# The last attention of a four-layer network: two passes made one slotted loop, with sums on TensorE and rounding on GpSimd

## The reference, cut to what matters

```python
q = (x @ Wq + bq).reshape(1, B * N, H, hd)
kv = (cond @ Wkv + bkv).reshape(1, -1, 2, H, hd)
q = _fq_sym(q * scale, axis=-1); k = _fq_sym(k, axis=-1); v = _fq_sym(v, axis=2)
attn = softmax(einsum('bhqd,bhkd->bhqk', q, k))
attn = _fq_unsigned(attn, axis=-1)      # s = max / 255, round(attn / s) * s
out = einsum('bhqk,bhkd->bhqd', attn, v)
return out.reshape(B, N, C) @ Wp + bp
```

## Time and profile before

| what | value |
|---|---|
| runs | 3636.0, 3638.04, 3641.99 us; median 3638.04 |
| the profiled execution's own time | 3633.23 us |
| its span, first to last instruction | 3631.5 us |
| first pass (from the first maximum) | 2589 to 2880 us |
| between the passes | 2880 to 2897 us |
| second pass | 2897 to 3197 us |
| end of the stage | 3220 us |

### The profile page before, as it was taken

The page is one execution under the profiler, slowest core; times in us unless marked ns, Lnnn a source line. Parts: engine busy times, 40 slices in busy tenths (PEclk is TensorE's granted clock), DMA queues, the critical chain, the costliest instruction groups (busy, mean ns, idle before and its releaser), DMA issues. The chain is left out here.

```text
span 3631.5 us, 49639 instructions
## 1 busy us (share of the span) xinstructions
PE 2993.6 (82%) x15375; PEld 1889.5 (52%) x15378; DVE 2276.1 (63%) x5414; ACT 1692.8 (47%) x3312; POOL 263.4 (7%) x323
## 2 busy tenths in 40 slices
PE   7887977787789999824999999726799899957899
PEld 4334645565567777612777777514211244434576
DVE  5664346767777777674444444477999866657532
ACT  4451224565655555411222222203699999934322
POOL 0010002111121111000000000040000000001200
PEclk9898987999999999956999999867655555567899
DMA  1002030000000000003000000001000000020000
GB/s 53 1 2 79 0 127 1 24 1 1 1 1 7 7 1 1 1 31 116 1 1 1 0 0 0 18 0 41 1 0 0 0 1 0 0 88 2 2 1 12
DMA packets 32878, 56.37 MB, mean 16 GB/s; under 512 B 5248, under 2 KB 24640, under 8 KB 30144
## 3 DMA queue, kind: packets, MB, share of 16 engines
q1 hardware_dynamic: 32704, 54.24, 4.3%
HBM read 52.99 MB, written 1.05 MB: 15 GB/s over the span
## 5 line engine op out<-in xcount | busy, mean ns | idle before, releaser
L2482 ACT ACTIVATE a_v_all<-psum,a_ln 128x1024 f32<-128x1024 f32 x256 | 283.9, 1114 | 14.7 <-PE psum L2421 9.3
L2536 DVE TENSOR_REDUCE a_half_max<-psum 128x1024 f32 x256 | 289.7, 1242 | 0.0
L2399 PE MATMUL psum<-a_ks,a_qs 96*128 (+1 forms) x512 | 263.6, 620 | 27.2 <-ACT psum L2468 16.8
L2468 ACT ACTIVATE psum<-psum,a_half_max 128x1024 f32<-128x1024 f32 x256 | 278.4, 1088 | 3.7 <-DVE a_half_max L2536 3.3
L2421 PE MATMUL psum<-a_qs,a_ks 99*128 (+1 forms) x512 | 263.6, 618 | 5.0 <-ACT a_qs L2474 1.2
L2559 DVE TENSOR_SCALAR a_probs<-a_v_all 128x1024 bf16<-128x1024 f32 x256 | 177.6, 694 | 122.6 <-ACT a_v_all L2482 110.2
L1581 ACT ACTIVATE a_normed<-psum,a_head_bias,a_head_scale 128x128 f32<-128x128 f32 x448 | 168.2, 457 | 160.5 <-DVE a_head_bias L1724 160.4
L1473 PE MATMUL psum<-a_probs_t,a_vals 128*128 128x256 f32 x768 | 202.5, 402 | 19.5 <-ACT a_probs_t L1599 19.5
L843 DVE SCALAR_TENSOR_TENSOR f_silu<-f_silu,psum 128x352 f32<-128x352 f32 (+2 forms) x88 | 50.4, 573 | 244.6 <-ACT f_silu L818 244.5
L1744 DVE TENSOR_REDUCE a_neg_max<-psum 128x2 f32<-128x512 f32 (+1 forms) x128 | 122.2, 955 | 124.4 <-PE psum L1453 123.9
L1453 PE MATMUL psum<-a_k_t,a_q_t 128*128 128x256 f32 (+1 forms) x512 | 194.1, 503 | 0.0
(11 more groups left out here) (465 smaller groups left out, 6407.1 us busy)
## 6 DMA issues: line engine op xcount, KB each, us to landing
a_w_raw<-in_L_xattn_wproj_dram SPq DMA_DIRECT2D x2, 2048.0 KB, 14.1
a_ctx_t<-in_ctx_t_dram SPq DMA_DIRECT2D x8, 512.0 KB, 5.4
f_w_silu<-in_L_ffn_gate_dram SPq DMA_DIRECT2D x1, 2112.0 KB, 9.6
f_w_mul<-in_L_ffn_up_dram SPq DMA_DIRECT2D x1, 2112.0 KB, 14.2
a_probs<-in_ctx_t_dram SPq DMA_DIRECT2D x4, 512.0 KB, 5.3
f_w_silu<-in_L_ffn_Wu_dram SPq DMA_DIRECT2D x1, 2048.0 KB, 8.0
f_w_mul<-in_L_ffn_Wg_dram SPq DMA_DIRECT2D x1, 2048.0 KB, 12.6
f_w_down<-in_L_ffn_Wd_dram SPq DMA_DIRECT2D x1, 2048.0 KB, 17.6
```

What stands on the lines that cost most here:

```text
L2399: mm = pe.matmul(core.bank(4 * (t % 2) + 2 * half + c), qs[0:KS, bass.ds(h * TOK + t * P, P)], ks[0:KS, bass.ds(h * CTX + (2 * half + c) * ...
L2468: act.activation(banks, banks, ACT.Exp, bias=half_max[:, half, at], accum_out=half_sums[:, half, at]).then_inc(summed, 1)
L2482: act.activation(exps[:, k % 4, :], core.bank(2 * (k % 2), 2), ACT.Exp, bias=ln255[:, :]).then_inc(exp_ready, 1)
L2536: v.tensor_reduce(half_max[:, half, bass.ds(h * NT + t, 1)], core.bank(4 * (t % 2) + 2 * half, 2), AX.X, ALU.max, negate=True).then_inc(ma ...
```

## The change

The two passes become one loop of 285 slots, written out in full. In slot s:

- TensorE makes the scores of pair s (128 queries by 1024 keys) into a ring of two double banks (banks 0 to 3). VectorE takes their negated maximum. ScalarE does not touch them.
- After a head's 16 pairs VectorE splits its 128 x 8 maxima into three parts. Two slots later TensorE transposes them at once (one transpose, through the same ring), VectorE copies the row block to `max_rows`, and SP writes it with three DMAs into `qs`.
- TensorE makes the logits of pair s - 21 (two key tiles by 512 queries) into two single banks (4 and 5), each as soon as the exponential before last has left it. ScalarE takes two exponentials of 128 x 512 in place of one of 128 x 1024, into a ring of 12 buffers.
- GpSimd rounds both to bf16 (128 x 1024 in one instruction), into a ring of 4.
- Every second slot TensorE takes a group of four key tiles. Four f32 matmuls with `one_row` (17 columns, a one in the last) add the exponentials' sums, and four bf16 matmuls with the values add the weighted values, all into bank 6, key tile u at the column tile 32u.
- After four groups (a chunk of 512 queries) ScalarE copies bank 6 to `out_t`; TensorE turns it with four f32 matmuls against `select` (which also adds the four column tiles); VectorE takes the reciprocal of the sum and multiplies twice.

GpSimd now also scales, rounds and clamps the values. ScalarE waits for that before its first exponential, since `v_all` and the exponentials share their space. Before the loop VectorE builds `select` and zeroes bank 6, and TensorE waits for that.

```diff
+        UNITS, PAIRS, TILES_PER = 12, 4, 4
+        PER = 2 * NT
+        LAG = PER + 5
+        SLOT_COUNT = LAG + H * PER + 8
+        RING, LOGITS, OUT, TURNED = 0, 4, 6, 7
...
 @block.sync
+                for h in range(H):
+                    sp.wait_ge(rows_kept, h + 1)
+                    if h >= 2:
+                        sp.wait_ge(ROWS_IN[h % 2], 48 * (h // 2))
+                    for part in range(3):
+                        sp.dma_start(qs[KS + part:KS + part + 1, h * TOK:(h + 1) * TOK].rearrange("a (t n) -> a t n", t=NT),
+                                     max_rows[part * NT:(part + 1) * NT, h % 2, :]).then_inc(ROWS_IN[h % 2], 16)
...
 @block.gpsimd
+                g.wait_ge(v_inv_ready, 1)
+                g.tensor_tensor(v_all[:, :, :], v_all[:, :, :], v_inv[:, :].unsqueeze(1).broadcast_to([P, KT, D]), ALU.mult).then_inc(v_step, 1)
+                g.wait_ge(v_step, 1)
+                g.tensor_scalar(v_all[:, :, :], v_all[:, :, :], ROUND, ROUND, ALU.add, ALU.subtract).then_inc(v_step, 1)
+                g.wait_ge(v_step, 2)
+                g.tensor_scalar(v_int[:, :, :, 0:DH], v_all[:, :, :].rearrange("p k (h d) -> p k h d", h=H), 127.0, -127.0,
+                                ALU.min, ALU.max).then_inc(v_ready, 1)
+                for m in range(H * PER):
+                    g.wait_ge(exp_ready, 2 * m + 2)
+                    at_least(g, weighted_done, (m - PAIRS) // 2 + 1)
+                    first = 2 * m % UNITS
+                    g.tensor_scalar(probs[:, m % PAIRS, :], exps[:, first:first + 2, :].rearrange("p u n -> p (u n)"),
+                                    ROUND, ROUND, ALU.add, ALU.subtract).then_inc(probs_ready, 1)
...
 @block.tensor
+                def rows(h):
+                    pe.wait_ge(ring_free, ring_use["rows", h] - 1)
+                    pe.wait_ge(parts_ready, h + 1)
+                    pe.transpose(ring(("rows", h)).bitcast(BF16)[0:3 * NT, 0:P], max_parts[:, h, :, :].rearrange("p s t -> p (s t)"),
+                                 core.ident_bf[:, :]).then_inc(ring_full, 1)
+
+                def logits(m):
+                    h, (c, j) = m // PER, divmod(m % PER, KT // 2)
+                    if m % PER == 0:
+                        pe.wait_ge(ROWS_IN[h % 2], 48 * (h // 2 + 1))
+                    for u in range(2):
+                        key = 2 * j + u
+                        at_least(pe, exp_ready, 2 * m + u - 1)
+                        pe.matmul(core.bank(LOGITS + u), ks[0:KM, h * CTX + key * P:h * CTX + (key + 1) * P],
+                                  qs[0:KM, h * TOK + c * QC:h * TOK + (c + 1) * QC], start=True, stop=True).then_inc(logits_full, 1)
+
+                def group(g):
+                    n, i = divmod(g, GROUPS)
+                    h, c = divmod(n, CH)
+                    if g == 0:
+                        pe.wait_ge(v_ready, 1)
+                    if i == 0:
+                        at_least(pe, out_kept, n)
+                    pe.wait_ge(exp_ready, TILES_PER * (g + 1))
+                    for u in range(TILES_PER):
+                        pe.matmul(core.bank(OUT)[32 * u:32 * u + W, :], one_row[:, :], exps[:, (TILES_PER * g + u) % UNITS, :],
+                                  start=(i == 0), stop=False, skip_group_check=True)
+                    pe.wait_ge(probs_ready, 2 * (g + 1))
+                    for u in range(TILES_PER):
+                        mm = pe.matmul(core.bank(OUT)[32 * u:32 * u + W, :], v_int[:, TILES_PER * i + u, h, :],
+                                       probs[:, (2 * g + u // 2) % PAIRS, u % 2 * QC:(u % 2 + 1) * QC],
+                                       start=False, stop=(i == GROUPS - 1), skip_group_check=True)
+                    mm.then_inc(weighted_done, 1)
+
+                for s in range(SLOT_COUNT):
+                    if s < H * PER:
+                        scores(s)
+                    if rows_slot(s) is not None:
+                        rows(rows_slot(s))
+                    if pair_at(s) is not None:
+                        logits(pair_at(s))
+                    if group_at(s) is not None:
+                        group(group_at(s))
+                    if chunk_at(s, 4) is not None:
+                        turn_heads(chunk_at(s, 4))
...
 @block.scalar
-                            act.activation(banks, banks, ACT.Exp, bias=half_max[:, half, at], accum_out=half_sums[:, half, at]).then_inc(summed, 1)
+                def exponential(m):
+                    for u in range(2):
+                        n = 2 * m + u
+                        act.wait_ge(logits_full, n + 1)
+                        at_least(act, weighted_done, (n - UNITS) // TILES_PER + 1)
+                        act.activation(exps[:, n % UNITS, :], core.bank(LOGITS + u), ACT.Exp, bias=ln255[:, :]).then_inc(exp_ready, 1)
...
 @block.vector
+                for s in range(SLOT_COUNT):
+                    if s < H * PER:
+                        maxima(s)
+                        if s == 2:
+                            scale_values()
+                        if s % PER == PER - 1:
+                            split(s // PER)
+                    if rows_slot(s) is not None:
+                        keep_rows(rows_slot(s))
+                    if chunk_at(s, 4) is not None:
+                        keep_heads(chunk_at(s, 4))
```

More of the change, by code:

```diff
@@ L2269, in layer3_attention @@
     CH = TOK // QC
-    GROUP = 2
-    GROUPS = KT // GROUP
+    W = DH + 1
     LEAST = 1e-8
@@ L2309, in layer3_attention @@
[L2309 to L2324, removed]
@@ L2392, in _ @@
                 pe.wait_ge(proj_free, TILES)
-                def scores(h, t):
-                    for half in range(2):
-                        at_least(pe, summed, 2 * (h * NT + t) + half - 3)
-                        for c in range(2):
-                            mm = pe.matmul(core.bank(4 * (t % 2) + 2 * half + c), qs[0:KS, bass.ds(h * TOK + t * P, P)],
-                                           ks[0:KS, bass.ds(h * CTX + (2 * half + c) * BANK, BANK)], start=True, stop=True)
-                        mm.then_inc(scores_ready, 1)
@@ L2438, in _, with scores @@
-                v_int_flat = v_int[:, :, :].rearrange("p k d -> p (k d)")
-                steps(pe, step)
+                pe.wait_ge(loop_ready, 1)
+                def scores(s):
+                    h, (t, half) = s // PER, divmod(s % PER, 2)
+                    n = ring_use["scores", s]
+                    if n >= 2:
+                        pe.wait_ge(ring_free, n - 1)
+                    for c in range(2):
+                        mm = pe.matmul(ring(("scores", s))[:, c * BANK:(c + 1) * BANK], qs[0:KS, h * TOK + t * P:h * TOK + (t + 1) * P],
+                                       ks[0:KS, h * CTX + (2 * half + c) * BANK:h * CTX + (2 * half + c + 1) * BANK], start=True, stop=True)
+                    mm.then_inc(ring_full, 1)
@@ L2577, in _ @@
-                v.drain()
-                for t in range(NT):
-                    one = heads[:, t, :].rearrange("p (h d) -> p h d", h=H)
-                    v.tensor_tensor(one, one, sums[:, :, t].unsqueeze(2).broadcast_to([P, H, DH]), ALU.mult).then_inc(out_ready, 1)
+                v.tensor_tensor(select[:, :], core.ident[:, 0:W], core.ident[:, 32:32 + W], ALU.add)
+                v.wait_ge(stack_free, 2 * TILES)
+                v.memset(core.bank(OUT), 0.0)
+                for u in range(2, TILES_PER):
+                    v.drain()
+                    last = v.tensor_tensor(select[:, :], select[:, :], core.ident[:, 32 * u:32 * u + W], ALU.add)
@@ new lines, in _ @@
+                for s in range(SLOT_COUNT):
+                    if s < H * PER:
+                        maxima(s)
[7 more added lines that the diff above has]
+                        keep_heads(chunk_at(s, 4))
+                v.drain().then_inc(out_ready, NT)
```

205 lines of the change are left out of this document (95 added, 110 removed).

## The result

The changed kernel takes 3989.7 us (median of 4 runs, 3988.4 to 3991.9) against 3638.0 before: 1.0966 times as long, 95% interval 1.0947 to 1.0985. The forecast was 3533, range 3455 to 3600, faster with 0.89: wrong in sign and outside its range. The profiled execution has a span of 3986.7 us.

The account below looks back on a forecast made before the run. VectorE filled the first pass, ScalarE most of the second. New stage: 2.7 + 27.7 + 416 + 32.6 + 19 + 3 + 3 + 4.2 = 508.2 against 612.8 us, 104.6 less; median 3533, range 3455 to 3600.

Parts of the forecast that it names:

- GpSimd's term: New loop, per slot: one GpSimd rounding of 128x1024 taken at 1.04 us plus 0.07 hand-over, bounds 1.04 and 2.34.
- rival 3: Loop: GpSimd's rounding costs like its two-input operation, 2.34 + 0.07, so every slot is 2.41; 3679 us, chance 0.07.
- The prediction's sentence on the Trainium skill: GpSimd rounding: some 2.6 cycles per element, estimated 2.2 us for 1024, against the move; one-or-two-operation bodies about one cycle.
- the stage: Last attention, first maximum to first transpose of the finished heads: 612.8 us before, forecast 508.2, so 104.6 less.
- Lead: Loop's start: 21 slots with maxima alone before the first logits, 27.7 us; GpSimd's value scaling, 17.7, covered.
- Chain of two slots: Loop: in-order queues from one odd exponential's end through TensorE to the next take 3.54 us, 1.77 a slot.
- Heads: Starts of 16 heads: split 1.15, waits for the row bank, and VectorE-GpSimd hindrance 0.6 each; 16 x 1.2 = 19 us.
- Turning a chunk: Finished chunks, 32 times: f32 transposes hold TensorE's queue some 0.5 us, costing 0.1 a chunk, 3 in all.
- rival 2: Values' sums: bf16 column tiles go one after the other, +0.66 every two slots, +84; 3617 us, chance 0.06.
- rival 4: TensorE through the loop: clock stays at 1.2 GHz, 195 us more; median 3728, chance 0.04.
- Rival 1: Loop: ScalarE is the bound at 1.54 us a slot, 181 less; median 3457, chance 0.13.
- the break-even: GpSimd's rounding in the loop: the change turns slower from 2.25 us a slot, an instruction of 2.18.

Follow-up runs that it names:

- experiment 1: Kernel before the change, with 26 GpSimd instructions of 128x1024 in various forms added beside the first pass to price each; 3632.7 us in its one run.
- experiment 2: Changed kernel with GpSimd copying the exponentials to bf16 in place of rounding them to whole numbers; 3577.4 us, ratio 0.9838.
- Experiment 9: Kernel with VectorE's rounding and scores between a pair's logits, with the values' add and subtract also moved from GpSimd to VectorE; 3543.7 us, ratio 0.9748.
- experiment 7: Changed kernel with the rounding on VectorE one slot later, and additionally the scores moved between the two logits of a pair; 3552.2 us, ratio 0.9770.
- experiments 6: Kernel with GpSimd copying instead of rounding, with the next scores moved between the two logits of a pair; 3569.8 us, ratio 0.9821.
- 8: Kernel with GpSimd copying instead of rounding, without TensorE's f32 set of sums (denominators from converted values); 3546.0 us, ratio 0.9743.
- experiment 5: Kernel with GpSimd copying instead of rounding, copying only 8 columns of each pair; 3545.7 us, ratio 0.9752.
- 3: Changed kernel with the rounding moved from GpSimd to VectorE, one slot later; 3563.9 us, ratio 0.9789.
- experiment 12: Copying kernel without sums, splits and heads' last product on GpSimd, values rounded on VectorE; then rows one slot, logits two slots later; 3442.7 us, ratio 0.9467.

## Why the prediction was wrong

**The step that failed is GpSimd's term**, "one input and constants resembles the cast: I take 1.04". It measured 3.63 alone (experiment 1), and one every 3.60 in the loop, outside bounds of 1.04 and 2.34 that both came from rows of other operations. Putting 3.60 in rival 3, whose mechanism is what happened, gives 3679 + 256 x (3.60 - 2.41) + 13 for the longer lead = 3997, against 3989.7. Its chance of 0.07 rested on those bounds, and its own price, 2.34 + 0.07, was too low as well.

The prediction's sentence on the Trainium skill, "GPSIMD Engine Reference", section 3.1, leaned the right way by luck. The section gives its 2.6 cycles for two inputs, and about one cycle per element for bodies of up to two operations, an estimate of 0.9 us for 1024 elements. The limits, multiply-and-add and the copies, at 1.04 to 1.05, lie near that; add-and-subtract at 3.63 and the single operations at 2.77 do not, and there the trace decides.

**The rest, judged by experiment 2, where GpSimd costs the 1.04 assumed:** the stage measures 556.6 us against 508.2.
- Lead: 40.3 against 27.7, +12.6. GpSimd's scaling was taken at 17.7 and "covered", to show from 4 us more. It took 26.45, mis-sized by the same operation (14.04). Its end, at 2629.2 in the changed kernel, was still 7.9 us before the first exponential; what it delayed was the first split in VectorE, whose steps waited beside it, and with that the turned row. Experiment 9 takes 6.4 off experiment 7's lead. (The lead's terms, as listed, add to 27.5, not 27.7.)
- Chain of two slots: 3.54 against 3.70. The mechanism holds: experiments 6 and 8 shorten it by 0.36 and by 0.87. Two sizes were off. The f32 set is 0.87, not 0.44: the earlier trace rows was read as eight sets of four, but an f32 matmul leaves two records, so 32 records are four sets. Exponentials back to back start 0.58 to 0.59 apart (the row of three in experiment 2), not 0.73. Together +0.43 and -0.29 make +0.14 of the 0.16 measured: one error hid two thirds of the other.
- Heads: hindrance was taken at 0.6 a head within bounds of 0 and 3.1; experiment 5 makes it 35.5 / 16 = 2.2. The nearest row had been one subtraction beside one select. Beside full copies the two conversions of a split take 1.05 and 0.86 instead of 0.17, and the chunks' product, not among the steps counted, 1.01 instead of 0.23, 32 times.
- Turning a chunk holds TensorE 0.8 to 0.96 us (eight records again), not 0.5.
- Right: the bf16 tiles lie side by side (four in 0.40), against rival 2; the clock is 0.95 to 1.00 in experiments 2, 3 and 5, against rival 4; the first maximum starts 2.4 us behind the reduction's end (2594.1), against 2.6; the end is 4.8 behind the last exponential's start.
- Rival 1, ScalarE as the bound: experiment 12 comes near it, with 1.47 us a pair and ScalarE busy for 88%.

What "would show it" named GpSimd over 90% busy, TensorE waiting before the bf16 set and small steps of over 1 us; all three came.

Open: why GpSimd's price depends so on the operations named. The runs give the prices and no reason for them.

## What to carry to other kernels

Before a step is moved to another engine, price that very operation there: rows of a cast and of a two-input operation, 1.04 and 2.34, lay on either side of the break-even and yet both below the 3.63 that it costs, 3.5 times the value taken. Small VectorE steps of 0.17 us beside GpSimd's instructions can each come to about 1 us, beside 1.04 and beside 3.63 alike (1.64 at most), and to 5.53 beside the long ones at the start, so count every one of them, and move them too. And when work is taken from TensorE, look at its waits again: with less to do, its clock fell behind them, and two slots of slack gave back what the removal had promised.

## What the runs showed that I had not expected

- On GpSimd, for 128x1024 f32: copy 1.04 us, both limits 1.04, multiply-and-add 1.05, add, subtract or multiply alone 2.77, add-and-max and add-and-subtract 3.63. VectorE does the last in 0.68.
- Steps of 8 columns on VectorE, two-input or conversions alike, lasted 2.52, 3.60 and 5.53 us beside GpSimd's long instructions at the start and 0.86 to 1.05 beside copies of 1.04. Beside the loop's roundings of 3.63 none lasted longer than 1.64: some of the casts ended 0.03 us behind a rounding's end, most of the other steps that were held about 1.05 us into a rounding, and the step of 5.53 ended 11.47 us into an instruction of 14.04. The maxima out of PSUM keep their 1.22.
- TensorE's granted clock fell from 1.00 to 0.50 behind its waits of 1.29 and 2.43 us, though it was busy again at once, and was back at 1.00 some 9 us after the end of the first and some 14 after the second. Without the sums this costs what they had cost. A wait alone does not do it: with the sums (experiment 2), waits of up to 1.5 us at the heads' starts left a clock of 0.97.
